# Cross-attention of a decoder layer: another order of the same work on all engines, another bank pair and no constant products in the output-only steps

## The reference, cut to what matters

```python
qk = jnp.einsum('bhqd,bhkd->bhqk', Q, K)
scores = qk / math.sqrt(dk)
mean_sim = scores.mean(axis=(-2, -1))
max_sim = scores.max(axis=-1).mean(axis=-1)
probs = jax.nn.softmax(scores, axis=-1)
entropy_proxy = jnp.var(probs, axis=-1, ddof=1).mean(axis=-1)
feats = jnp.stack([mean_sim, max_sim, entropy_proxy], axis=-1)
hidden = jax.nn.gelu(_linear(feats, w1, b1), approximate=False)
hidden = jax.nn.gelu(_linear(hidden, w2, b2), approximate=False)
log_t = jnp.clip(_linear(hidden, w3, b3), LOG_T_MIN, LOG_T_MAX)
t = jnp.exp(log_t)[..., None]
attn = jax.nn.softmax(qk / (2.0 * t), axis=-1)
out = jnp.einsum('bhqk,bhkd->bhqd', attn, V)
```

## Time and profile before

| | us |
|---|---|
| median of 3 runs (1714.52 to 1722.27) | 1720.15 |
| the profiled execution, its own time | 1719.28 |
| its span, first to last instruction | 1717.5 |
| self-attention | about 480 |
| cross-attention, from there to the last `residual` at 1160.89 | about 681 |
| feed-forward part | about 556 |

### The profile page before, as it was taken

One profiled execution on the slowest core, in us unless ns is written; L12 is line 12 of the kernel. 1 busy time (PEld: TensorE's weight loads), 2 busy tenths in 40 slices (PEclk: granted clock), 3 DMA queues, 4 the chain that ended last, 5 costly groups with the idle time before them and its releaser, 6 DMA issues. The chain is left out here.

```text
span 1717.5 us, 42620 instructions
## 1 busy us (share of the span) xinstructions
PE 1642.8 (96%) x14336; PEld 1223.2 (71%) x14336; DVE 1235.7 (72%) x2888; ACT 926.2 (54%) x2189; POOL 880.2 (51%) x1006
## 2 busy tenths in 40 slices
PE   6999999999978999999999999897999999999998
PEld 2555555555546666666666666557999999999998
DVE  5887777777646767766677776436878878787886
ACT  3555545555433666666566666545454545545452
POOL 3444455544446767776677777412433434343342
PEclk9999999999958999998999999788999999999999
DMA  4000000000000000000000000100000000000000
GB/s 123 13 3 2 1 1 1 1 1 1 6 5 4 7 7 7 6 7 6 6 7 7 7 7 5 43 2 1 11 6 9 6 9 6 9 9 6 9 6 13
DMA packets 27869, 16.62 MB, mean 10 GB/s; under 512 B 6193, under 2 KB 25586, under 8 KB 27762
## 3 DMA queue, kind: packets, MB, share of 16 engines
q1 hardware_dynamic: 27762, 15.23, 3.2%
HBM read 9.97 MB, written 4.19 MB: 8 GB/s over the span
## 5 line engine op out<-in xcount | busy, mean ns | idle before, releaser
L1555 POOL TENSOR_TENSOR ff_zz<-ff_zt 128x256 f32<-128x256 f32 x32 | 37.5, 1173 | 318.2 <-DVE ff_zt L1759 318.2
L278 POOL TENSOR_TENSOR sa_KM<-sa_HQK,sc_headmask 128x512 fp32r<-128x512 f32 x64 | 66.7, 1042 | 235.6 <-ACT sa_HQK L318 235.6
L964 ACT ACTIVATE xa_P<-xa_SK 77x1024 f32<-77x1024 f32 x128 | 130.2, 1017 | 98.1 <-PE xa_SK L1287 97.9
L1623 ACT ACTIVATE ff_SG<-bank 128x512 f32<-128x512 f32 x128 | 76.6, 599 | 189.3 <-PE bank L1836 189.3
L1749 DVE TENSOR_TENSOR ff_GL<-ff_GU,ff_GH 128x512 fp32r<-128x512 f32 x128 | 148.6, 1180 | 27.2 <-ACT ff_GH L1628 27.2
L323 ACT ACTIVATE sa_P<-sa_SK 128x1024 f32<-128x1024 f32 x128 | 131.5, 1028 | 59.1 <-PE sa_SK L515 59.1
L409 DVE TENSOR_REDUCE sa_mx<-sa_SQ 128x8 f32<-128x1024 f32 x128 | 156.7, 1224 | 7.6 <-PE sa_SQ L515 5.3
L890 POOL TENSOR_TENSOR xa_QMH<-xa_QBH,xc_headmask 128x512 fp32r<-128x512 f32 x64 | 72.6, 1135 | 151.2 <-ACT xa_QBH L954 151.2
L1901 PE MATMUL bank<-fh_r,ff_GH 128*128 128x256 f32 x512 | 149.2, 292 | 0.0
L1834 PE MATMUL bank<-ff_ZH,fh_b 128*128 128x256 f32 x512 | 146.2, 286 | 0.0
L1903 PE MATMUL bank<-fh_r,ff_GL 128*128 128x256 f32 x512 | 144.5, 282 | 0.0
(11 more groups left out here) (259 smaller groups left out, 5398.3 us busy)
## 6 DMA issues: line engine op xcount, KB each, us to landing
xa_shift<-xa_row SPq DMA_DIRECT2D x256, 2.0 KB
out<-X SPq DMA_DIRECT2D x64, 64.0 KB, 1.5
cx<-ctx SPq DMA_DIRECT2D x64, 38.5 KB
sa_shift<-sa_mT SPq DMA_DIRECT2D x64, 8.0 KB, 1.8
X<-x SPq DMA_DIRECT2D x1, 768.0 KB, 6.7
xa_E<-L_ffn_B SPq DMA_DIRECT2D x2, 256.0 KB, 3.7
xa_E<-down_a SPq DMA_DIRECT2D x1, 512.0 KB, 4.4
X<-x SPq DMA_DIRECT2D x1, 256.0 KB, 2.9
```

What stands on the lines that cost most here:

```text
L964: nc.scalar.activation(P[0:TC, (2 * b + h) % 4, :], SK[0:TC, :], ACT.Exp).then_inc(p_ready, 1)
```

## The change

It reorders the calls in the step loop of PE, ACT and DVE; renames which row group serves which four heads (`CROSS_ORDER`); puts `by_key(b, 1)` of items 57 to 63 into two `SQ` banks, so that there a half waits only for the half before the last; and drops the filler of the output-only steps except the last of them. The diff, cut to its core (first the banks and rows, then the loops of ACT and DVE, then PE):

```diff
+CROSS_ORDER = (2, 1, 3, 0)
...
+        ALONE = B - LAG
+        def by_key_banks(b, h):
+            return SQ[:, 0:1024] if b >= ALONE and h == 1 else SK[:, 0:1024]
...
-                for g in range(QUADS):
+                for place, g in enumerate(ORDER):
                     sp.dma_start(shift[32 * g:32 * g + 1, b % 2].bitcast(F32),
-                                 row[JH * g:JH * g + JH].bitcast(F32)).then_inc(m_row[b % 2], 16)
+                                 row[JH * place:JH * place + JH].bitcast(F32)).then_inc(m_row[b % 2], 16)
...
-                nc.scalar.activation(P[0:TC, (2 * b + h) % 4, :], SK[0:TC, :], ACT.Exp).then_inc(p_ready, 1)
+                nc.scalar.activation(P[0:TC, (2 * b + h) % 4, :], by_key_banks(b, h)[0:TC], ACT.Exp).then_inc(p_ready, 1)
...
 
             for n in STEPS:
                 r = mlp_round(n)
-                if real(n - LAG):
-                    exps(n - LAG, 0)
                 if real(n - LAG + 1):
                     scaled(n - LAG + 1)
+                if r is not None:
+                    gelu1(r)
+                if real(n - LAG) and r is None:
+                    exps(n - LAG, 0)
                 if real(n + 2):
                     xcT_copy(n + 2)
                 if r is not None:
-                    gelu1(r)
+                    gelu2(r)
                 if real(n - LAG - 1):
                     o_copy(n - LAG - 1)
-                if r is not None:
-                    gelu2(r)
+                if real(n - LAG) and r is not None:
+                    exps(n - LAG, 0)
                 if real(n):
                     mT_copy(n)
                 if real(n + 2):
                     qkv_copy(n + 2)
+                if r is not None:
+                    inverse_t(r)
+                if real(n):
+                    exp_e(n)
+                if real(n - LAG - 1):
+                    onT_copy(n - LAG - 1)
                 if real(n - LAG):
                     exps(n - LAG, 1)
-                if r is not None:
-                    inverse_t(r)
-                if real(n - LAG - 1):
-                    onT_copy(n - LAG - 1)
-                if real(n):
-                    exp_e(n)
...
 
             for n in STEPS:
                 r = mlp_round(n)
-                if real(n - LAG - 2):
-                    residual(n - LAG - 2)
                 if n % 2 == 1 and real(n - 2):
                     inverse_sums((n - 3) // 2)
                 if real(n - 1):
                     sum_e(n - 1)
+                if real(n - LAG - 2):
+                    residual(n - LAG - 2)
                 if real(n - LAG + 1):
                     low(n - LAG + 1)
                 if real(n):
                     row_max(n)
+                if r is not None:
+                    bound(r)
                 if real(n - LAG - 2):
                     stats(n - LAG - 2)
-                if r is not None:
-                    bound(r)
-                if real(n - LAG - 1) and r is None:
+                if real(n - LAG - 1):
                     norm(n - LAG - 1)
+                if real(n + 3):
+                    layernorm(n + 3)
                 if real(n + 2):
                     cast(n + 2)
-                if r is not None and real(n - LAG - 1):
-                    norm(n - LAG - 1)
+                if r is not None:
+                    factors(r)
                 if real(n - 1):
                     sum_e2(n - 1)
-                if real(n + 3):
-                    layernorm(n + 3)
...
-            def scores(b, first_head, last_head, part, start, stop):
-                g = first_head // JH
+            def scores(b, first, last, part):
+                g = ORDER[first // JH]
                 rows = slice(32 * g, 32 * g + 32)
                 queries, keys = PARTS[part]
-                at = first_head // 6 * 512 + first_head % 6 * TC
-                j = first_head % JH
-                n = last_head - first_head
+                at = first // 6 * 512 + first % 6 * TC
+                j = first % JH
+                n = last - first
                 return mm(SQ[:, at:at + n * TC], queries[rows, b % QRING],
-                          keys[rows, b % 2, j:j + n].rearrange("c j k -> c (j k)"), start=start, stop=stop,
-                          skip_group_check=True)
+                          keys[rows, b % 2, j:j + n].rearrange("c j k -> c (j k)"), start=(part == 0 and n == JH),
+                          stop=(part == 2), skip_group_check=True)
...
-                    scores(b, 0, 4, part, part == 0, part == 2)
-                    scores(b, 8, 12, part, part == 0, part == 2)
-                    last = scores(b, 12, 16, part, part == 0, part == 2)
+                    scores(b, 0, 4, part)
+                    last = scores(b, 8, 12, part)
                 last.then_inc(outer_ps, 1)
 
             def scores_inner(b):
+                scores(b, 12, 16, 0)
                 pe.wait_ge(outer_ps, b + 1)
                 for part in range(3):
-                    scores(b, 4, 6, part, False, part == 2)
-                    last = scores(b, 6, 8, part, False, part == 2)
+                    if part > 0:
+                        scores(b, 12, 16, part)
+                    scores(b, 4, 6, part)
+                    last = scores(b, 6, 8, part)
...
-            def by_key(b, h, between=None):
-                need(pe, p_ready, 2 * b + h)
+            def by_key(b, h, between):
+                need(pe, p_ready, 2 * b + h if b <= ALONE and h == 0 else 2 * b + h - (b >= ALONE))
+                if b == ALONE and h == 1:
+                    pe.wait_ge(e1_ready, B)
+                banks = by_key_banks(b, h)
...
-                    mm(bank(SK, a), pick[:, r // 32], shift[:, b % 2].rearrange("c j t -> c (j t)"),
+                    mm(bank(banks, a), pick[:, r // 32], shift[:, b % 2].rearrange("c j t -> c (j t)"),
                        start=True, stop=False)
+                between()
                 for part, (keys, queries) in enumerate(((HK, QMH), (HK, QML), (LK, QMH))):
                     for a, rows, _ in quads:
-                        last = mm(bank(SK, a), keys[rows, slot(b)],
+                        last = mm(bank(banks, a), keys[rows, slot(b)],
                                   queries[rows, b % 2].rearrange("c j t -> c (j t)"), start=False, stop=(part == 2))
-                    if part == 0 and between is not None:
-                        between()
...
                 r = mlp_round(n)
                 if n == 2:
                     pe.wait_ge(pick_set, 1)
-                if n == B:
-                    pe.wait_ge(e1_ready, B)
-                if real(n - LAG - 2):
-                    project(n - LAG - 2)
+
+                def project_last():
+                    if real(n - LAG - 2):
+                        project(n - LAG - 2)
+
+                def subtract():
+                    if real(n):
+                        subtract_max(n)
+
                 if 2 <= n < LAG:
                     filler(SK[:, 0:512], 4)
                 if real(n - LAG):
-                    by_key(n - LAG, 0)
+                    by_key(n - LAG, 0, project_last)
+                else:
+                    project_last()
                 if real(n):
                     scores_outer(n)
-                if real(n - LAG - 1):
-                    pv(n - LAG - 1, 1)
+                    scores_inner(n)
                 if r is not None:
                     mlp1(r, n)
                 if real(n + 2):
                     xc_transpose(n + 2)
-                if real(n):
-                    scores_inner(n)
+                if r is not None:
+                    mlp2(r)
+                if real(n - LAG - 1):
+                    pv(n - LAG - 1, 1)
+                elif 2 <= n < LAG:
+                    filler(SK[:, 512:1024], 3)
+                if r is not None:
+                    mlp3(r)
                 if real(n + 2):
                     qkv(n + 2)
-                if r is not None:
-                    mlp2(r)
-                elif real(n - LAG - 1):
-                    if n >= B:
-                        filler(SQ[:, 0:512], 6)
+                if real(n - LAG - 1):
+                    if n >= B + LAG:
+                        filler(SQ[:, 1024:1536], 6)
                     o_transpose(n - LAG - 1, r)
-
-                def maxima():
-                    if real(n):
-                        max_transpose(n)
-                    if r is not None:
-                        mlp3(r)
-
+                if real(n):
+                    max_transpose(n)
                 if real(n - LAG):
-                    by_key(n - LAG, 1, maxima)
+                    by_key(n - LAG, 1, subtract)
                 else:
                     if 2 <= n < LAG:
-                        filler(SK[:, 512:1024], 6)
-                    maxima()
-                if r is not None and real(n - LAG - 1):
-                    o_transpose(n - LAG - 1, r)
-                if real(n):
```

(3 more changed lines are left out.)

6 lines of the change are left out of this document (3 added, 3 removed).

## The result

The change makes the kernel slower: median 1796.16 us of 4 runs (1776.40 to 1803.75), against 1720.80 of 4 (1714.52 to 1722.27) for the kernel before on the same chip; ratio 1.041, interval 1.031 to 1.050. The forecast of 1743 had the sign right and the size wrong; the time lies outside its range.

The account below looks back on a forecast made before the run. A ring of waits across PE, DVE and ACT, no full engine, was taken to set the step. +21.4 + 16 - 14 - 1 = +22.4 on 1719.3 gave 1741.7, plus 0.9 to the median: 1743, range 1710 to 1768.

Parts of the forecast that it names:

- The plain step: Cross-attention step without MLP: exps and by-key work enter the ring of waits, 8.59 to 9.0 us, 41 times, +16.8.
- the MLP step: Cross-attention step with MLP: exps(n-7, 0) behind o_copy and the Exp table load, 11.47 to 11.8 us, 14 times, +4.6.
- Term +21.4: Steps 9 to 63 at full clock: the longer steps without and with MLP together, +21.4 us.
- Side by side: Step's scores: outer scores run beside by-key products in other row groups, which together take 0.97 us, despite the program-order rule.
- The clock: Steps 9 to 63: 5 us of half clock in each of 14 groups at 0.35, against 7.7 before; +16, 0 to +30.
- The output-only steps: Steps at the end: from 7.10 to about 5.9 us with the second half in SQ; -14, between -8 and -19.
- The first steps: Start of the cross-attention: fewer fillers, Gelu load hidden once, steps 7 and 8 on the longer ring; -1, give or take 4.
- half clock in steps without MLP: Rival, steps without MLP: 3 us of half clock in every second step, 32 more, 1775 us; chance 0.12.
- the clock stays as it is: Rival, steps 9 to 63: no more half clock than before, so the +16 is 0, about 1727 us; chance 0.17.
- The faster rival: Rival, inner scores: scores, wait and transposes close up by 0.3, step 8.75, about 1707 us; chance 0.10.
- strict order of products: Rival, TensorE: outer scores stand behind the by-key products, +0.5 a step, 27 in all, 1770 us; chance 0.03.
- the change is not what it says: Rival, step order: inner scores still wait long for outer, or exps is not behind exp_e; near 1720 us; chance 0.02.

Follow-up runs that it names:

- b_expslate: Kernel before with one part of the change: on ScalarE exp_e(n) ahead of onT_copy and exps(n-7, 1); 1831.1 us, ratio 1.056 to 1.068.
- a_tail: Changed kernel with the six constant products of 512 columns back in every output-only step; 1764.8 us, ratio 1.022 to 1.031.
- a_gap: Changed kernel with three constant products of 512 columns at each step's start, in the wait for exps; 1742.8 us, ratio 1.006 to 1.019.
- a_dense: Changed kernel with three constant products of 512 columns per step, ahead of project, where TensorE has no wait; 1781.6 us, ratio 1.027 to 1.036.
- c_final: c_swap without the three constant products in MLP steps; 1776.4 us, ratio 1.025 to 1.034.
- c_swap: c_best with onT_copy behind exps(n-7, 1) on ScalarE instead of ahead of it; 1725.0 us, ratio 1.002 to 1.006.
- c_thin: c_swap with two more constant products of 512 columns in each MLP step, ahead of mlp2; 1709.3 us, ratio 0.994 to 0.997.
- b_fast: b_banks with gelu1 and gelu2 moved up on ScalarE and mlp2 ahead of qkv on TensorE; 1777.8 us, ratio 1.029 to 1.037.
- b_banks: Kernel before with by_key(b, 1) of items 57 to 63 in two SQ banks, constant products kept; 1718.5 us, ratio 0.998 to 1.002.
- a_side: Changed kernel with eight constant products of 128 columns in each MLP step, ahead of mlp2; 1803.9 us, ratio 1.045 to 1.060.
- c_best: a_gap with MLP steps' first by-key half moved behind mlp3 and four constant products per output-only step; 1740.6 us, ratio 1.010 to 1.013.

## Why the prediction was right in sign and wrong in size

- **The plain step, forecast 8.99, measured 8.98; the MLP step, forecast 11.8, measured 11.77.** Term +21.4, measured +20.2 at full clock. The places agree within 0.15: shift products forecast at E+1.17, measured E+1.14; end of the maxima at 5.85 and 6.00; `mT_copy` done at 6.68 and 6.82; start of the subtraction 6.88 and 6.87. That the sum agrees to 0.01 is in part luck: shift products and `project` take 1.33 instead of 1.15, and the subtraction starts 0.05 behind `mT_copy` instead of 0.2. b_expslate, which the same account put at 9.75, came out at 9.75.
- **Side by side.** The outer scores again start right behind the first by-key products of the other row groups (989.09 and 989.11), with four more by-key products ahead of them in the program. The trace does not agree with the strict order that the Trainium skill, "TensorE: Matmul & The Clock Gate", Part 3, states, and no time was lost to it.
- **The clock. This is the step that failed:** "I take 5 us of half clock in each of the 14 groups at 0.35". The price was right: 63.1 us lost over 184 is 0.34 per us, and 563.9 - 533.0 = 30.9 over 91 in a_tail's execution is 0.34 too. The amount was not: 184 / 14 = 13 us per group, mostly 17 in one piece. Term +16 with an upper bound of +30, measured 63.1 - 7.7 = +55.4 in the profiled execution. I had carried over from the earlier trace rows that the clock is back within a step or so of the fall, as in the step of 1002.79 after the MLP step of 991.31, and read the one long piece there (13.7, in the step of 811.35) only for its price. In the new order TensorE falls as often, 12 times, but mostly stays at half clock through the MLP step's end and nearly the whole next step. I had priced the pauses and not asked how much work per time is left for the clock to come back on. a_gap and a_dense show that more work in every step shortens the stay, c_final, c_swap and c_thin in the MLP step: 188, 48 and 0 us of half clock with no, three and five constant products there. Why the clock stays down so long in the changed order is open beyond that: b_fast has 184 us on a ring as short as before.
- **The output-only steps** failed in the same way. "Denser steps lose less" and the 6 us given back took it for granted that dropping the six constant products does not cost the clock. It does: 9.88 a step at clock 0.50, tail +6.5 instead of -14. At full clock the step is 6.24 (forecast 5.9), and with four products the tail is 53.0 to 53.7 in four kernels, 13.3 to 14.0 less than before; so the size stands, if the clock is held. The mechanism was half right: that with one bank pair each half waits for the other's `exps` is not what held the step at 7.10, since b_banks takes this wait away and stays there.
- **The first steps**: -1 forecast, +2.3 measured, inside the 4 given. In all +22.4 was forecast and +84.4 measured: 39 of the missing 62 lie in the clock of steps 9 to 63 and 20 in the output-only steps.
- **The rivals.** The nearest was half clock in steps without MLP (1775, chance 0.12): its place, a plain step in which TensorE waits, is where the time went, mostly in the one step behind the MLP step (13.73 instead of 8.98), though most of those falls begin in the MLP step and run on into it. That the clock stays as it is fell; so did strict order of products and that the change is not what it says. The faster rival needed a plain step of 8.75 and was wrong on it.

The profiled execution lies 7.6 above the median; by the 1776.4 of another execution, at a mean clock of 0.929 instead of 0.908, the miss would still be 33.

## What to carry to other kernels

When a reorder makes a ring of waits longer on a kernel whose clock already falls now and then, the few tenths per step can be the small part of the bill, 20 of 84 us here: ask in each step whether the clock can come back after a fall, not only what a fall costs. Constant products are work that can bring it back: dropping them, or leaving a step without them, is to be priced like adding a wait, and putting two or three where the trace shows a fall is worth trying, with a trace after each try, since several of the guesses made here missed (a_side, b_fast, c_best, c_final). A forecast for such a kernel should have a range as wide as the half clock of its whole stretch, since the same instructions lost 31 us in one execution and 63 in another.

## What was not expected of the hardware

- The same program part (steps 9 to 63 of the changed kernel and of a_tail) had 184 us of half clock in one execution and 91 in another, and the pattern can lock: from 878 on seven groups in a row fell at the same place for 17.1 us each.
- The clock fell although TensorE's waits for `exps` in that stretch are at most 1.3 us long and it counts as busy for 549.3 of 596.1 us. The Trainium skill, "TensorE: Matmul & The Clock Gate", Part 1, says that the clock follows how busy TensorE has been recently. a_dense agrees, in that added products keep the clock up with the pauses left in place (31 us of half clock instead of 184); b_fast, with the same products as the kernel before at nearly the same step lengths, shows that the amount alone does not tell it.
- Unused products made the whole kernel faster: c_thin against c_final, 67 us.
